# Last step of the pre-normalizations moved from VectorE to ScalarE, with squares, a conv tap, a mix and the rotary part rewritten in the third stage

## The reference, cut to what matters

```
x = x + LN(attention 0 (LN(x)))        # causal, one head
x = x + LN(gated MLP   (LN(x)))
x = x + LN(4 x [local + linear attention, MLP] (LN(x)))   # each with its own pre-norms ln1, ln2
x = x + LN(soft mixture of experts (LN(x)))
x = x + LN(attention 2 (LN(x)))        # 16 heads of 8
x = x + LN(gelu MLP    (LN(x)))
x = x + LN(block 3     (LN(x)))
x = x + LN(top-k experts (LN(x)))      # bf16 at its end

LN(x) = (x - mean) / sqrt(var + 1e-5)          rms(x) = x / sqrt(mean(x^2) + eps)

block 3:  xm = m0*x + m1*x;  n = rms(xm)
          value, gate = n @ in_proj;  value = silu(conv4(value) + b)
          y = scan(value, xm @ B, xm @ C) ... ;  xm += s * (y*silu(gate)) @ out_proj
          xm += s * relu(rms(xm) @ fc)^2 @ proj
          xa = a0*xm + a1*x;  n = rms(xa);  q, k = rms(n @ q_w), rms(n @ k_w)
          q, k = rotary(q), rotary(k)     # [a*cos + b*sin, -a*sin + b*cos] on halves of 4
          xa += s * attention(q, k, v) @ o_w
          xa += s * relu(rms(xa) @ fc)^2 @ proj
```

## Time and profile before

| | |
|---|---|
| runs of the kernel before | 3852.84, 3858.43, 3865.88 us (median 3858.43) |
| the profiled execution | 3854.58 us, of which the span is 3852.8 us |
| granted TensorE clock, mean of that execution | 0.864 of full speed |
| busy: PE, PEld | 2967.9 us (77%), 2348.8 us (61%) |
| busy: DVE, ACT, POOL | 2519.0 us (65%), 1670.4 us (43%), 475.3 us (12%) |
| chain that ended last, by engine | PE 48%, DVE 40%, ACT 8%, issue 3%, POOL 1% |
| DMA | 27.96 MB, mean 7 GB/s |

### The profile page before, as it was taken

The page is one execution under the profiler, slowest core; times in us unless marked ns, Lnnn a source line. Parts: engine busy times, 40 slices in busy tenths (PEclk is TensorE's granted clock), DMA queues, the critical chain, the costliest instruction groups (busy, mean ns, idle before and its releaser), DMA issues.

```text
span 3852.8 us, 76103 instructions
## 1 busy us (share of the span) xinstructions
PE 2967.9 (77%) x31950; PEld 2348.8 (61%) x31950; DVE 2519.0 (65%) x7052; ACT 1670.4 (43%) x3492; POOL 475.3 (12%) x451
## 2 busy tenths in 40 slices
PE   6788877778887848878875878957777798585895
PEld 3466665456666548767764765846666486474564
DVE  5666555665655578889897666567565845756337
ACT  3444444444444447777773443223434332251222
POOL 1100000110000022222222011110010211001000
PEclk7889888888988969989997998977989899697887
DMA  2000000000000010000000000000000000001000
GB/s 85 1 1 1 1 1 1 1 1 1 1 1 1 1 50 7 6 9 6 7 1 12 3 2 1 2 0 2 2 2 3 1 2 1 1 3 44 1 1 23
DMA packets 13541, 27.96 MB, mean 7 GB/s; under 512 B 784, under 2 KB 9232, under 8 KB 12688
## 3 DMA queue, kind: packets, MB, share of 16 engines
q1 hardware_dynamic: 13200, 23.10, 1.7%
HBM read 21.00 MB, written 2.10 MB: 6 GB/s over the span
## 4 chain that ended last, share of the span: by engine, by line
PE 48%; DVE 40%; ACT 8%; issue 3%; POOL 1%; DMA 0%; SPq 0%; DVEq 0%; POOLq 0%; ACTq 0%
PE ps L312 6%; DVE LN L1916 5%; DVE LN L258 4%; PE ps L303 3%; DVE RS L237 3%; PE ps L1274 3%; PE ps L1794 3%; PE ps L369 3%; PE ps L456 2%; PE ps L277 2%; DVE M L472 2%; DVE LN L1929 2%; DVE M L613 2%; PE ps L1285 2%; PE ps L1738 1%
## 5 line engine op out<-in xcount | busy, mean ns | idle before, releaser
L285 ACT COPY LN<-ps 128x512 f32<-128x512 f32 (+4 forms) x592 | 303.6, 547 | 827.7 <-PE ps L277 267.5
L265 POOL TENSOR_TENSOR RS<-RS,MISC 128x4 f32<-128x4 f32 x216 | 220.4, 1020 | 2295.4 <-DVE RS L249 1725.4
L277 PE MATMUL ps<-cons,LN 128*128 128x128 f32 x672 | 149.5, 368 | 396.7 <-DVE LN L258 198.9
L277 PEld LDWEIGHTS ps<-cons,LN 128*128 128x128 f32 x672 | 100.6, 184 | 456.1 <-DVE LN L258 169.7
L472 DVE TENSOR_REDUCE M<-ps 128x6 f32<-128x768 f32 x256 | 241.8, 955 | 139.7 <-PE ps L456 95.1
L1916 DVE TENSOR_TENSOR LN<-LN 128x1024 f32<-128x1024 f32 (+2 forms) x192 | 219.8, 1145 | 24.9 <-ACT LN L285 13.5
L369 PE MATMUL ps<-LN 32*128 32x256 f32 x1024 | 185.7, 437 | 53.1 <-DVE LN L508 32.0
L613 DVE TENSOR_REDUCE M<-ps 128x12 f32<-128x1536 f32 x64 | 112.3, 1755 | 162.5 <-PE ps L359 162.2
L1794 PE MATMUL ps<-LN,wAB 128*128 128x128 f32 x1024 | 149.1, 308 | 75.4 <-ACT LN L285 74.9
L372 PE MATMUL ps<-LN 32*128 32x256 f32 x1024 | 202.9, 475 | 0.8 <-DVE M L472 0.8
L303 PE MATMUL ps<-LN,wAB 128*128 128x512 f32 x384 | 198.5, 648 | 3.2 <-DVE LN L933 2.9
(11 more groups left out here) (340 smaller groups left out, 7452.3 us busy)
## 6 DMA issues: line engine op xcount, KB each, us to landing
wAB<-wb SPq DMA_DIRECT2D x16, 256.0 KB, 2.5
LN<-wd SPq DMA_DIRECT2D x8, 512.0 KB, 7.2
wAB<-wa SPq DMA_DIRECT2D x1, 3840.0 KB, 15.9
wCs<-wc SPq DMA_DIRECT2D x1, 2336.0 KB, 11.2
XA<-xin SPq DMA_DIRECT2D x8, 256.0 KB, 7.6
y<-XA SPq DMA_DIRECT2D x8, 256.0 KB, 2.3
wAB<-wb SPq DMA_DIRECT2D x1, 1024.0 KB, 4.9
wAB<-wm SPq DMA_DIRECT2D x1, 1024.0 KB, 4.9
```

Of the source, the lines that this page charges most:

```text
L265: pool.e.tensor_tensor(c.r[:, 40:44], c.r[:, 36:40], mhalf, ALU.pow).then_inc(*c.G.inc((k, "rstd")))
L277: ins = pe.e.transpose(ps[:, n * 128:(n + 1) * 128], src[:, n, :], ident)
L285: act.e.copy(dst, ps).then_inc(*c.A.inc(named(k, done)))
```

## The change

1. Pre-normalizations: VectorE keeps only the statistics (`dve_stats`). GpSimd computes the reciprocal deviation as before, and for the layernorm form also shift = -mean * rstd in two more instructions of 128 x 4. ScalarE applies both, tile by tile, as four Identity activations with a scale and (layernorm) a bias per partition (`act_norm`). TensorE's transposes wait for ScalarE in place of VectorE. There are 144 pre-normalizations: 80 in the first stage (16 before attention 0 and its MLP, 64 in the four layers), 16 in the two input passes, 48 in the third stage (32 of these in the rms form).
2. Third stage: the squares of the relu MLPs are done by ScalarE from SBUF (64 instructions); the first conv tap too, from PSUM (16). The first mix of block 3 is one instruction with the factors rm0 + rm1, summed once. Squares, their sums and the rotary products are done over all four tiles at once. The copy of a transpose to SBUF stands one round later in ScalarE's queue, at the head of the step that uses it.
3. After the mixture, ScalarE divides by the softmax sums (32 instructions).

```diff
+        def dve_stats(dve, c, k, src, rms=False, eps=1e-5):
+            next(dve_norm(dve, c, k, src, src, rms, eps))
+
+        def act_norm(act, c, k, src, dst, rms=False):
+            act.wait_ge(c.G, (k, "rstd" if rms else "shift"))
+            for i in range(4):
+                rs, sh = c.r[:, 40 + i:41 + i], c.r[:, 44 + i:45 + i]
+                if rms:
+                    ins = act.e.activation(dst[:, i, :], src[:, i, :], ACT.Identity, scale=rs)
+                else:
+                    ins = act.e.activation(dst[:, i, :], src[:, i, :], ACT.Identity, scale=rs, bias=sh)
+                ins.then_inc(*c.A.inc((k, "normed", i)))
+
+        def pool_norm_shift(pool, c, k):
+            mean = c.r[:, 24:32].rearrange("p (i c) -> p i c", c=2)[:, :, 0]
+            yield from pool_norm(pool, c, k, False)
+            pool.wait_ge(c.G, (k, "rstd"))
+            pool.e.tensor_tensor(c.r[:, 44:48], c.r[:, 40:44], mean, ALU.mult).then_inc(*c.G.inc())
+            pool.wait_ge(c.G)
+            pool.e.tensor_tensor(c.r[:, 44:48], c.r[:, 44:48], mone, ALU.mult).then_inc(*c.G.inc((k, "shift")))
+            yield
+
...
-            pe.wait_ge(c.D, (k, "normed", 3))
+            pe.wait_ge(c.A, (k, "normed", 3))
...
-            yield from dve_norm(dve, c, k, Z, v["XN"])
+            dve_stats(dve, c, k, Z)
+            yield
...
         def dve_relu_mlp(dve, c, k, v, rep):
-            yield from dve_norm(dve, c, k, v["Z"], v["YN"], rms=True, eps=EPS)
-            yield
+            dve_stats(dve, c, k, v["Z"], rms=True, eps=EPS)
+            yield
+            yield
+            yield
+            yield
+            scaled(dve, c, k, "sum", "y", v["Z"], rep, v["tmp"])
+
+        def act_relu_mlp(act, c, k, v):
+            yield
+            act_norm(act, c, k, v["Z"], v["YN"], rms=True)
+            yield
+            act_copy(act, c, k, v["XT"], c.ps[0][:, :], "tr", "xT")
             for j in range(4):
-                dve.wait_ge(c.A, (k, "relu", j))
-                dve.e.scalar_tensor_tensor(v["h3"][:, j, :], c.ps[j % 2][:, :], 0.0, v["h3"][:, j, :], ALU.max,
-                                           ALU.mult).then_inc(*c.D.inc((k, "h", j)))
+                h = v["h3"][:, j, :]
+                act.wait_ge(c.P, (k, "up", j))
+                act.e.activation(h, c.ps[j % 2][:, :], ACT.Relu).then_inc(*c.A.inc((k, "relu", j)))
                 if j % 2:
-                    yield
-            scaled(dve, c, k, "sum", "y", v["Z"], rep, v["tmp"])
-
-        def act_relu_mlp(act, c, k, v):
-            yield
-            act_copy(act, c, k, v["XT"], c.ps[0][:, :], "tr", "xT")
-            yield
-            for j in range(4):
-                act.wait_ge(c.P, (k, "up", j))
-                act.e.activation(v["h3"][:, j, :], c.ps[j % 2][:, :], ACT.Relu).then_inc(*c.A.inc((k, "relu", j)))
-                if j % 2:
+                    for jj in (j - 1, j):
+                        h = v["h3"][:, jj, :]
+                        act.wait_ge(c.A, (k, "relu", jj))
+                        act.e.activation(h, h, ACT.Square).then_inc(*c.A.inc((k, "h", jj)))
                     yield
...
-            mixed(dve, c, (g, "l3m"), Z, XN, wv("rm0"), XN, wv("rm1"), v["tmp"])
+            dve.wait_ge(DD[LANES], "rm")
+            dve.e.tensor_tensor(Z, XN, rep4(wv("rm0")), ALU.mult).then_inc(*c.D.inc(((g, "l3m"), "mixed")))
...
-                dve.e.tensor_scalar(v["VT"][:, n, :], v["RAW"][:, n, :], w4[:, 3:4], wv("convb")[:, n:n + 1], ALU.mult,
-                                    ALU.add).then_inc(*c.D.inc())
...
-            rb, sq = v["rb"], v["sq"]
-            for t in range(4):
-                dve.wait_ge(c.A, (k, t // 2, "qkv"))
-                b_ = sq[:, 160 * (t % 2):160 * (t % 2) + 160]
-                dve.e.tensor_tensor(b_, QK[:, t, :], QK[:, t, :], ALU.mult).then_inc(*c.D.inc())
-                dve.wait_ge(c.D)
-                dve.e.tensor_reduce(rb[:, 20 * t:20 * t + 20], b_.rearrange("p (h d) -> p h d", d=8), X_AX,
-                                    ALU.add).then_inc(*c.D.inc())
+            dve_stats(dve, c, k, Z, rms=True, eps=EPS)
+            yield
+            yield
+            yield
+            rb, sq, un = v["rb"], v["sq"], v["un"]
+            dve.wait_ge(c.A, (k, 1, "qkv"))
+            dve.e.tensor_tensor(sq, QK, QK, ALU.mult).then_inc(*c.D.inc())
+            dve.wait_ge(c.D)
+            dve.e.tensor_reduce(rb, sq.rearrange("p t (h d) -> p (t h) d", d=8), X_AX, ALU.add).then_inc(*c.D.inc())
             dve.wait_ge(c.D)
             dve.e.tensor_scalar(rb, rb, 0.125, EPS, ALU.mult, ALU.add).then_inc(*c.D.inc((k, "ms")))
             yield
...
             dve.wait_ge(c.D)
             qk = QK.rearrange("p t (h d) -> p (t h) d", d=8)
             dve.e.tensor_tensor(qk, qk, rb.unsqueeze(2).to_broadcast([128, 80, 8]), ALU.mult).then_inc(*c.D.inc())
+            q8, s8, u8 = (x.rearrange("p t (h d) -> p t h d", d=8) for x in (QK, sq, un))
+
+            def turn(name, o, n):
+                x = wv(name).rearrange("p (t d) -> p t d", d=8)[:, :, o:o + n]
+                return x.unsqueeze(2).to_broadcast([128, 4, 20, n])
+
+            dve.wait_ge(c.D)
+            dve.e.tensor_tensor(s8, q8, turn("cos8", 0, 8), ALU.mult)
+            dve.e.tensor_tensor(u8[:, :, :, 0:4], q8[:, :, :, 4:8], turn("sin8", 0, 4), ALU.mult)
+            dve.e.tensor_tensor(u8[:, :, :, 4:8], q8[:, :, :, 0:4], turn("sin8", 4, 4), ALU.mult).then_inc(*c.D.inc())
+            dve.wait_ge(c.D)
+            dve.e.tensor_tensor(QK, sq, un, ALU.add).then_inc(*c.D.inc())
+            dve.wait_ge(c.D)
             for t in range(4):
-                j = t % 2
-                q3 = QK[:, t, :].rearrange("p (h d) -> p h d", d=8)
-                cos = wv("cos")[:, 4 * j:4 * j + 4].unsqueeze(1).to_broadcast([128, 20, 4])
-                sin = wv("sin")[:, 4 * j:4 * j + 4].unsqueeze(1).to_broadcast([128, 20, 4])
-                xa, xb = q3[:, :, 0:4], q3[:, :, 4:8]
-                r3 = sq[:, 0:160].rearrange("p (h d) -> p h d", d=8)
-                u3 = sq[:, 160:320].rearrange("p (h d) -> p h d", d=8)
-                dve.wait_ge(c.D)
-                dve.e.tensor_tensor(r3[:, :, 0:4], xa, cos, ALU.mult)
-                dve.e.tensor_tensor(u3[:, :, 0:4], xb, sin, ALU.mult)
-                dve.e.tensor_tensor(r3[:, :, 4:8], xb, cos, ALU.mult)
-                dve.e.tensor_tensor(u3[:, :, 4:8], xa, sin, ALU.mult).then_inc(*c.D.inc())
-                dve.wait_ge(c.D)
-                dve.e.tensor_tensor(xa, r3[:, :, 0:4], u3[:, :, 0:4], ALU.add)
-                dve.e.tensor_tensor(xb, r3[:, :, 4:8], u3[:, :, 4:8], ALU.subtract).then_inc(*c.D.inc())
                 kr4 = v["KR"][:, t, :].rearrange("p (g r d) -> p g r d", g=4, d=8)
                 k3_ = QK[:, t, 128:160].rearrange("p (g d) -> p g d", d=8)
-                dve.wait_ge(c.D)
-                dve.e.tensor_copy(kr4, k3_.unsqueeze(2).to_broadcast([128, 4, 4, 8])).then_inc(
-                    *(c.D.inc((k, "roped")) if t == 3 else c.D.inc()))
+                ins = dve.e.tensor_copy(kr4, k3_.unsqueeze(2).to_broadcast([128, 4, 4, 8]))
+            ins.then_inc(*c.D.inc((k, "roped")))
...
                 act.wait_ge(c.P, (k, "val", n))
+                act.e.activation(v["VT"][:, n, :], c.ps[n][:, :], ACT.Identity, scale=wv("convw")[:, 4 * n + 3:4 * n + 4],
+                                 bias=wv("convb")[:, n:n + 1])
                 act.e.copy(v["RAW"][:, n, :], c.ps[n][:, :]).then_inc(*c.A.inc((k, "raw", n)))
...
         def dve_out(dve, c, g):
-            dve.wait_ge(DD[LANES], "rls")
+            dve.wait_ge(c.A, ((g, "so"), "mean"))
             YG = YA.rearrange("p b m e -> p (b m) e")[:, 4 * g:4 * g + 4, :]
+            yield from dve_post(dve, c, (g, "so"), XG[g], YG)
+
+        def act_out(act, c, g):
+            YG = YA.rearrange("p b m e -> p (b m) e")[:, 4 * g:4 * g + 4, :]
+            act.wait_ge(DD[LANES], "rls")
             for i in range(4):
                 t = 4 * g + i
-                dve.e.tensor_scalar(YG[:, i, :], YG[:, i, :], LS[:, t % 2, t // 2:t // 2 + 1], None, ALU.mult).then_inc(
-                    *c.D.inc())
-            yield from dve_post(dve, c, (g, "so"), XG[g], YG)
+                ins = act.e.activation(YG[:, i, :], YG[:, i, :], ACT.Identity, scale=LS[:, t % 2, t // 2:t // 2 + 1])
+            ins.then_inc(*c.A.inc(((g, "so"), "mean")))
+            yield
```

106 lines of the change are left out of this document (70 added, 36 removed).

## The result

The changed kernel takes 3912.32 us (median, 3906.65 to 3916.00), the kernel before 3857.17 us in the same rounds: a ratio of 1.0139, with a 95% interval of 1.0117 to 1.0161, some 54 us slower. The forecast was 3766 us, its range 3700 to 3840.

The account below looks back on a forecast made before the run. No engine is busy throughout, so the chain of waits was taken to bound the kernel, with VectorE's runs on it. Savings 35 + 5 - 4 + 15 + 10 + 3 + 24 = 88 us from 3854.6 gave 3766 us, range 3700 to 3840.

Parts of the forecast that it names:

- First stage, 35 us: First stage: moving 80 pre-normalizations from VectorE to ScalarE was to save 35 us.
- the two terms behind it: First stage: 60 us off VectorE's chain, 23 us back as 18% of ScalarE's 128 us of new work, 2 us more exposed.
- Prices: Four normalizing activations on ScalarE: 1.65 us, 1.3 in the rms form; the shift's multiplications on GpSimd at most 0.317 each.
- Output of the mixture, 5 us: After the mixture: moving the divisions, 7 us on VectorE in eight groups, to ScalarE was to save 5 us.
- The two input passes, 4 us longer: Input passes: ScalarE becomes the pacer with norm and copy, 2 us more each, 4 in all.
- Before the scan, 15 us less: Third stage before the scan: VectorE loses norm, mix and tap work of 29 us over 8 lanes; 15 us was taken.
- the "half" that was taken: Before the scan: half of VectorE's 29 us relief was counted, since ScalarE gets norm, taps and a later copy.
- Relu MLPs, 10 us less, and 3 after attention: Third-stage relu MLPs: 1.3 us less per round over four rounds and two halves, 10 us; after attention 3 us less.
- a full round through ScalarE of 15.0 us: Relu MLPs: one new round, summed piece by piece through ScalarE, was put at 15.0 us against 14.3 before.
- Rotary, 24 us: Third-stage rotary part: wide instructions cut 8.0 us per lane to 4.8, 26 us over 8 lanes; 24 was taken.
- The one on the slower side: Whole kernel: transposes wait for ScalarE's activations; at 55% of 340 us exposed against 149 taken off, 3893 us; chance 0.07.
- The signs named in advance: Signs of error: transposes waiting longer for ScalarE than for lines 256 and 258, MLP rounds over 16 us, norms over 2.1, more table loads.

Follow-up runs that it names:

- run 7: The kernel of run 2 with the 80 normalizations of the first stage also put back on VectorE: 3786.84 us.
- run 2: The changed kernel with the third stage's norms back on VectorE and its copies a round earlier, squares still on ScalarE: 3753.00 us.
- runs 5 and 6: Third-stage copies: 5, the changed kernel with them a round earlier, norms unmoved, 3827.11 us; 6, run 2 with them a round later, 3817.80 us.
- run 11: The kernel of run 2 with squares, sums and rotary part again tile by tile: 3773.15 us.

## Why the prediction was wrong

- **First stage, 35 us: the size was right by luck.** It is 34 us by run 7, but the two terms behind it were both far too small. VectorE's part of the chain there fell by 128 us, not 60: with the norms, more of VectorE's run left the path than their own line. ScalarE's part grew by 70 us, not 23: its work grew by 123 us (569.96 to 692.75), so 57% of it ended on the path, not 18%. TensorE's part grew by 17. The two errors cancelled.
- **Prices: right.** The overlap of neighbours was read a little low, 0.085 us where four of 0.783 in 2.79 us share 0.34 over three seams, which is 0.11; on four activations that is 0.1 us.
- **Output of the mixture, 5 us: right** (-5.1). **The two input passes, 4 us longer: wrong but small** (-0.8 and -1.0).
- **The second layer's input: missing.** The sum held nothing for these eight groups, 25.7 us.
- **Before the scan, 15 us less: measured 21 more** (+16.6 and +4.4). Without late copies and late norms (run 2) the stretch of MLP and gates gives 14.2, and this mostly from the mix (11.9) and hardly from the tap; the "half" that was taken was the wrong way of cutting it. The "copy one round later", which the forecast named there as one of the things in ScalarE's queue, was the costliest edit of all: 65 us by itself and 85 beside the new norms, while it adds no work. The sum held no wait for what stands behind it.
- **Relu MLPs, 10 us less, and 3 after attention: measured +28.7 and +26.4.** This is the step that failed most: 1.3 us less per round rested on a full round through ScalarE of 15.0 us, with lighter rounds around it. The full round is 19.0 us, and none of the rounds became shorter. The sum of the round took one late copy at its price, 0.6 us. It left out the second lane's late copy, and the products and copies of q, k and v behind it (3.2 us with the issue), and it counted the second set of products at 1.9 us, half of eight products in the earlier trace rows, where it ran at a granted clock of 0.54 after a wait of 2.20 us (1.7 us more). Over the third stage TensorE's products wait 122 us for copies, a wait that the forecast put at nothing. That this wait is one of place is shown by runs 5 and 6, which move copies and nothing else.
- **Rotary, 24 us: right in size** (17 to 20 by run 11), hidden in part in the changed kernel (-8.5) by late copies ahead of the first lane.
- **The rivals.** The one on the slower side, at 3893 us and a chance of 0.07, came nearest. Its mechanism, ScalarE's in-order queue as the pacer, is the one found; its place was not: it was put everywhere, with a threshold of 44% exposed against 149 us taken off. In the first stage 57% of ScalarE's new work was exposed, and yet the stage is shorter, since VectorE gave back 128 us and not 60; in the third stage VectorE's part of the chain fell by 199 us, but ScalarE's grew by 153 and TensorE's by 141. Against it the forecast had argued that "most transposes stand a round later"; in the second layer's input they stand in the norm's own round.
- **The signs named in advance**: full rounds over 16 us (19.0) came true. The other did not: TensorE's transposes wait less for norms than before.

```profile
L300 PE MATMUL ps<-cons,LN 128*128 128x128 f32 x672 | 141.0, 351 | 315.5 <-ACT LN L272 206.7 <-ACT LN L270 81.7 <-DVE LN L1608 23.9
```

288.4 us for lines 272 and 270, against 330.6 before:

```profile
L277 PE MATMUL ps<-cons,LN 128*128 128x128 f32 x672 | 149.5, 368 | 396.7 <-DVE LN L258 198.9 <-DVE LN L256 131.7 <-DVE LN L1562 48.1
```

The wait moved to the products behind the copies (122 us against 1.5), so a sign that looks at one wait can be passed by a kernel in which another has grown. Of the amounts named, VectorE's busy time fell by 227 us, not 284, ScalarE's rose by 262, not 300, and the input passes did not become longer. The stretch from the last scan to the attention became 10 us longer per half (28.7 - 8.5 = 20.2 in both), not 15 shorter.

The rule of the Trainium skill (ScalarE: Activation LUTs, Rules for kernel authors) to keep relu, max, add and mul on VectorE, weighed in the forecast for squares and norms, gives VectorE's speed in bf16 as its reason. For this kernel's f32 it is not borne out as a rule on time: per instruction the norm is dearer on ScalarE (487 against 341 ns), yet moving the squares gains 26 us in one order and loses 45 in another.

## What to carry to other kernels

When work moves to another in-order queue, its price and the engine's idle share say little. Write out, for each place, what stands ahead of the new instruction in that queue, when its input is ready and who waits for it, and do the same for every instruction that the move pushes back: copies put a round later, with no work added, cost 65 us here. If the input is ready a round earlier, put the instruction there, ahead of the older lanes' evacuations; but try it stage by stage, since the same step cost 191 us in the first stage here. And the length of a round must be written out from the new order, piece by piece, with each copy and what waits behind it.

## What the runs showed that was not expected

The sign of an edit depends on another edit: the squares on ScalarE gain 26 us or lose 45 us by where norms and copies stand. The time of a product depends on the order too: the same four products took 1.73 us at a granted clock of 1.00 and 3.58 at 0.54, 4 us apart in one round. The price of an activation of 128 x 128 with scale and bias from memory is 487 ns, with the scale alone 396; four in a row take 1.64 and 1.29 us.
